# Third attention of an eight-stage kernel: the mask written into PSUM by ScalarE instead of added by 16 identity products a batch

## The reference, cut to what matters

```python
def _L2_xattn_ref(x, cond, mask, wq, bq, wk, bk, wv, bv, wo, bo):
    q = _w8a8_linear(x, wq, bq)            # 8-bit quantised rows times quantised weights
    k = cond @ wk.T + bk ; v = cond @ wv.T + bv      # 16 heads of 16 channels
    scores = jnp.einsum('bhnd,bhld->bhnl', q, k) * inv_sqrt_d + mask[:, None]
    attn = jax.nn.softmax(scores, axis=-1)
    o = jnp.einsum('bhnl,bhld->bhnd', attn, v)
    return _w8a8_linear(o, wo, bo)

x = x + jnp.tanh(g_xattn[2]) * _L2_xattn_ref(_layernorm(x, axis=-1), ctx_2048, mask_BxSxS2_ff0, ...)
```

## Time and profile before

| what | value |
|---|---|
| median of 3 runs | 1387.62 us (1384.13 to 1390.42) |
| profiled execution | 1374.32 us, its span 1372.5 us |
| TensorE, share of the span busy | 83% |
| VectorE | 65% |
| ScalarE | 39% |
| GpSimd | 32% |
| mean granted TensorE clock | 0.939 of 2.4 GHz |
| stage 4, first mask product to last batch's last value work | 742.8 us to about 975 us |

### The profile page before, as it was taken

One profiled execution on the slowest core, in us unless ns is written; L12 is line 12 of the kernel. 1 busy time (PEld: TensorE's weight loads), 2 busy tenths in 40 slices (PEclk: granted clock), 3 DMA queues, 4 the chain that ended last, 5 costly groups with the idle time before them and its releaser, 6 DMA issues.

```text
span 1372.5 us, 34438 instructions
## 1 busy us (share of the span) xinstructions
PE 1144.5 (83%) x12364; PEld 902.6 (66%) x12364; DVE 897.8 (65%) x2468; ACT 534.2 (39%) x1013; POOL 434.1 (32%) x943
## 2 busy tenths in 40 slices
PE   4889898984783888879987999998465799999998
PEld 2667676663771444446665676766354699999998
DVE  3656575665555898856665777777556666666665
ACT  2455554554552676630001333322125333333332
POOL 2444465647858887210011111113222100000000
PEclk8999999996995999989998999999789899999999
DMA  5332332403666454310000000000116100000000
GB/s 186 109 110 79 123 100 92 161 19 115 207 197 152 144 149 131 101 62 1 0 0 24 25 15 23 15 23 0 39 29 191 48 2 17 1 15 0 9 6 16
DMA packets 91469, 93.86 MB, mean 68 GB/s; under 512 B 10276, under 2 KB 83380, under 8 KB 90588
## 3 DMA queue, kind: packets, MB, share of 16 engines
q1 hardware_dynamic: 85500, 78.24, 18.3%
q0 software_dynamic: 4992, 13.66, 3.3%
q10 hardware_dynamic: 864, 0.43, 0.1%
HBM read 56.76 MB, written 35.53 MB: 67 GB/s over the span
## 4 chain that ended last, share of the span: by engine, by line
PE 60%; DVE 16%; issue 9%; ACT 6%; DMA 4%; POOL 3%; SPq 1%; DVEq 1%; ACTq 0%; POOLq 0%
PE psum L2336 5%; PE psum L1387 4%; PE psum L1389 4%; PE psum L1388 4%; PE psum L1012 3%; DMA PT<-xs 2%; DVE mx L782 2%; PE psum L2091 2%; ACT PT L2034 2%; ACT ext L2043 2%; PE psum L1405 2%; PE psum L1407 2%; PE psum L944 2%; PE psum L1406 2%; PE psum L2076 2%
## 5 line engine op out<-in xcount | busy, mean ns | idle before, releaser
L685 POOL TENSOR_SCALAR veps<-mv 128x1 f32<-128x1 f32 x112 | 26.8, 239 | 684.9 <-DVE mv L1255 367.4
L1387 PE MATMUL psum<-xnTh,w7h 128*128 128x256 f32 x512 | 147.1, 287 | 0.0
L1389 PE MATMUL psum<-xnTh,w7l 128*128 128x256 f32 x512 | 145.8, 285 | 0.0
L1388 PE MATMUL psum<-xnTl,w7h 128*128 128x256 f32 x512 | 145.7, 285 | 0.0
L782 DVE TENSOR_REDUCE mx<-psum 128x6 f32<-128x960 f32 (+3 forms) x80 | 80.7, 1008 | 68.8 <-PE psum L980 67.7
L1464 ACT ACTIVATE sil<-psum 128x256 f32<-128x256 f32 x128 | 49.3, 385 | 189.4 <-PE psum L1389 189.4
L1487 DVE TENSOR_TENSOR hTf<-sil,psum 128x256 f32<-128x256 f32 x128 | 53.8, 420 | 97.7 <-ACT sil L1464 97.6
L1389 PEld LDWEIGHTS psum<-xnTh,w7l 128*128 128x128 f32 x512 | 99.1, 193 | 0.0
L1387 PEld LDWEIGHTS psum<-xnTh,w7h 128*128 128x128 f32 x512 | 98.8, 193 | 0.0
L1388 PEld LDWEIGHTS psum<-xnTl,w7h 128*128 128x128 f32 x512 | 98.7, 193 | 0.0
L869 ACT ACTIVATE PT<-psum 128x1024 f32<-128x1024 f32 x64 | 65.5, 1024 | 71.0 <-PE psum L1000 71.0
(11 more groups left out here) (359 smaller groups left out, 3183.3 us busy)
## 6 DMA issues: line engine op xcount, KB each, us to landing
xs<-qpad SPq DMA_DIRECT2D x17, 1024.0 KB, 5.1
ctxT<-in_ctxT SPq DMA_DIRECT2D x48, 128.0 KB, 2.2
ext<-qscr SPq DMA_DIRECT2D x96, 64.0 KB
w_raw<-in_w SPq DMA_DIRECT2D x16, 384.0 KB, 3.3
arena<-in_w SPq DMA_DIRECT2D x4, 1280.0 KB, 9.9
PT<-xs SPq DMA_DIRECT2D x39, 128.0 KB, 2.6
ys<-yt SPq DMA_DIRECT2D x39, 128.0 KB, 2.8
q_parts<-kscr SPq DMA_DIRECT2D x66, 64.0 KB, 2.2
```

The lines of the kernel that those rows point to most:

```text
L1387: MM(o, wh, xnTh[:, s, c], start=(c == 0), stop=False)
L1388: MM(o, wh, xnTl[:, s, c], start=False, stop=False)
L1389: t = MM(o, wl, xnTh[:, s, c], start=False, stop=(c == NC - 1))
```

## The change

TensorE no longer has `add_mask`, GpSimd no longer splits the mask, and the identity in the product's type is gone. ScalarE gets `lay_mask(s, which, k)`, a copy of the mask, spread over 8 heads, from SBUF into two banks at once. It is called four times a batch: twice after the maxima are taken (`which` 1, the transposed mask, for the second scores of the same batch), and twice right after the exp of the same banks (`which` 0, for the first scores of the next batch). So that the score products with `start=False` add to what ScalarE wrote, four products of identities with `start=True` go over banks 4 to 7 once at the start of the stage. The flag `msk` now counts the four copies, and the transfers for batch b+2 wait for the fourth of batch b.

```diff
-        mskp = sb("mskp", [128, 2, 2, 2, T], F32R)
-        ident_r = sb("ident_r", [128, 128], F32R)
-        sb("pad", [128, 896])
+        sb("pad", [128, 2048])
...
-                    sp.wait_ge(F("msk").sem, F("msk").at(b, 2))
+                    sp.wait_ge(F("msk").sem, F("msk").at(b, 4))
...
-            def split(b, s, turn, wait=True):
...
-                P.tensor_copy(mskp[:, s, :, 0], msk[:, s]).then_inc(F("msk").sem, 1)
-                pool.wait_ge(F("msk").sem, F("msk").at(b, 1))
-                P.tensor_tensor(mskp[:, s, :, 1], msk[:, s], mskp[:, s, :, 0].bitcast(F32), ALU.subtract).then_inc(F("msk").sem, 1)
...
+            pool_stage(4, pool)
...
+            def lay_mask(s, which, k):
+                A.copy(bank(4 + 2 * k, 2).rearrange("p (h t) -> p h t", t=T), msk[:, s, which].unsqueeze(1).to_broadcast([128, 8, T])).then_inc(F("msk").sem, 1)
+
             def first():
+                act.wait_ge(wprep_pe, 2)
+                wait("msk_loaded0", 0, 32)
+                for k in range(2):
+                    lay_mask(0, 0, k)
                 copy_x(0)
...
             def body(p, b, n, s, turn, turn_b):
                 if p is not None:
                     copy_values(p)
+                for k in range(2):
+                    wait("mx", b, k + 1)
+                    lay_mask(s, 1, k)
                 wait("st", b, 1)
+                if n is not None:
+                    wait(f"msk_loaded{1 - s}", turn, 32)
                 for k in range(2):
                     A.activation(PT[:, 1024 * k:1024 * (k + 1)], bank(4 + 2 * k, 2), ACT.Exp).then_inc(F("p").sem, 1)
                     if k == 0 and n is not None:
                         copy_x(n)
+                if n is not None:
+                    for k in range(2):
+                        wait("p", b, k + 1)
+                        lay_mask(1 - s, 0, k)
                 if n is not None:
                     copy_k(n, 1 - s)
...
-            def add_mask(s, which, k):
-                for r in (2 * k, 2 * k + 1):
-                    for part in range(2):
-                        MM(bank(4 + r), ident_r[:], mskp[:, s, which, part].unsqueeze(1).to_broadcast([128, 4, T]), start=(part == 0), stop=False, skip_group_check=True)
...
             def first():
+                for r in range(4):
+                    t = MM(bank(4 + r), identb[:], identb[:].unsqueeze(1).to_broadcast([128, 4, 128]), start=True, stop=True)
+                t.then_inc(wprep_pe, 1)
                 transpose_x(0)
...
                 wait("msk", b, 2)
-                for k in range(2):
-                    wait("p", b, k - 1)
-                    add_mask(s, 0, k)
                 wait("k", b, 2)
...
-                for k in range(2):
-                    wait("mx", b, k + 1)
-                    add_mask(s, 1, k)
                 wait("mparts", b, 4)
...
                 wait("mxT", b, 1)
+                wait("msk", b, 4)
...
-                V.tensor_copy(ident_r[:], ident[:]).then_inc(G.sem, 1)
-                dve.wait_ge(G.sem, 2)
```

More of the change, by code:

```diff
@@ L379, in bass_program @@
         ff_flags(3)
-        stage_flags(4, LN + [("ctx_loaded0", 16, 0), ("ctx_loaded1", 16, 0), ("msk_loaded0", 32, 0), ("msk_loaded1", 32, 0), ("msk", 2, 0), ("quant", 6, 0), ("xT_psum", 1, 0), ("xT", 1, 0), ("q_psum", 1, 0), ("k_psum", 1, 0),
+        stage_flags(4, LN + [("ctx_loaded0", 16, 0), ("ctx_loaded1", 16, 0), ("msk_loaded0", 32, 0), ("msk_loaded1", 32, 0), ("msk", 4, 0), ("quant", 6, 0), ("xT_psum", 1, 0), ("xT", 1, 0), ("q_psum", 1, 0), ("k_psum", 1, 0),
                              ("qdve", 3, 0), ("k", 2, 0), ("qT_psum", 1, 0), ("qT", 1, 0), ("sq", 1, 0), ("mx", 2, 0), ("mparts", 4, 0),
-                             ("mxT_psum", 1, 0), ("mxT", 1, 0), ("st", 1, 0), ("p", 2, 2), ("pv", 1, 0), ("pvc", 1, 0), ("pvT", 1, 0), ("rden", 1, 0), ("on", 1, 0),
+                             ("mxT_psum", 1, 0), ("mxT", 1, 0), ("st", 1, 0), ("p", 2, 0), ("pv", 1, 0), ("pvc", 1, 0), ("pvT", 1, 0), ("rden", 1, 0), ("on", 1, 0),
                              ("oquant", 6, 0), ("oT_psum", 1, 0), ("oT", 1, 0), ("y", 1, 0), ("fin", 2, 0)])
@@ L2142, in s4_sp @@
                     sp.wait_ge(F("k_psum").sem, F("k_psum").at(b, 1))
-                    sp.wait_ge(F("msk").sem, F("msk").at(b, 2))
+                    sp.wait_ge(F("msk").sem, F("msk").at(b, 4))
                     load(i * 2 + (u + 2), u)
         def s4_pool(pool):
-            F = lambda n: f[4, n]
-            P = nc.gpsimd
-            rs = rstd_step(4, pool)
-            def split(b, s, turn, wait=True):
[L2153 to L2157, removed]
-                P.tensor_copy(mskp[:, s, :, 0], msk[:, s]).then_inc(F("msk").sem, 1)
-                pool.wait_ge(F("msk").sem, F("msk").at(b, 1))
-                P.tensor_tensor(mskp[:, s, :, 1], msk[:, s], mskp[:, s, :, 0].bitcast(F32), ALU.subtract).then_inc(F("msk").sem, 1)
[L2162 to L2169, removed]
+            pool_stage(4, pool)
         def s4_dve(dve):
@@ L2588, in _ @@
                 A.copy(k_parts[:, s, :, :, 48:64], k_const[:].rearrange("p (c h r) -> p c h r", c=2, h=HK0)).then_inc(gates_ready, 1)
-            give(act, [(4, "p")])
             s0_act(act)
@@ L2646, in _ @@
                 V.tensor_scalar(fb[:], fb[:], gates[:, 6:7], None, ALU.mult).then_inc(G.sem, 1)
-                dve.wait_ge(G.sem, 3)
+                dve.wait_ge(G.sem, 2)
                 s5_dve(dve)
```

## The result

| kernel | median | range | ratio to before (95% interval) |
|---|---|---|---|
| before | 1386.62 us (4 runs) | 1384.13 to 1390.42 | |
| changed | 1414.08 us (4 runs) | 1406.83 to 1414.72 | 1.0193 (1.0150 to 1.0237) |

The change makes the kernel slower by 27 us, 1.9%. A fifth run of the changed kernel, not among the four, took 1419.18 us.

The account below looks back on a forecast made before the run. Stage 4's chain of waits, 13.70 us a batch, was taken as the bound. Constant-clock terms of +1.3 and a falling clock of +21 took the profiled 1374.3 to 1397 us, the median from 1387.6 to 1410; range 1384 to 1431.

Parts of the forecast that it names:

- Price of a copy: Each 128x1024 float32 mask copy by ScalarE from SBUF into PSUM, four a batch: taken as 1.02 us.
- both bounds: Limits for one ScalarE mask copy: 0.59 us from a half-size copy below, 1.2 us from VectorE's pass above.
- the rival that needed a copy of 0.7 or less: Clock holds and ScalarE's copy into PSUM is cheap: total falls by about 8 us, 1377 at 0.6; chance 0.08.
- Leg A: Stage 4, end of second scores to first maxima: 7.8 us in place of 7.34, +0.45 a batch.
- Leg B: Stage 4, first maxima to end of next second scores: 6.1 us at constant clock, -0.25 a batch.
- The sum at constant clock: Both legs over the stage's batches plus the first batch: +6.8, -4.0 and -1.5, making +1.3 us.
- the -1.5: First batch of stage 4: scores stand behind the query's 0.59 us copy, not 2.12 of mask; -1.5 us.
- The clock: Stage 4: granted clock falls in four batches of five, 1.4 us a batch on average, 21 us in all.
- The pause: TensorE idle between the values and the turned maxima: 3.0 us in every batch of stage 4.
- the smaller gap: TensorE idle before the output product, waiting for ScalarE's output copy: 1.2 us a batch, given no cost.
- That the clock holds (1389): Stage 4 keeps full clock through all or nearly all batches: +1.3 us, 1389, between 1384 and 1395; chance 0.19.
- That it stays low throughout (1434): Clock falls and stays low over most of stage 4: 3.0 us a batch, 45 more, 1434; chance 0.1.

Follow-up runs that it names:

- both gaps filled: Changed kernel plus thrown-away TensorE products, eight before the turned maxima and four before the output product: 1375.38 us on another chip, 1.0002 of before.
- the table of two by two: Four kernels against before: ScalarE copies, pause open +27.5 us, filled with eight products +0.5; no copies or mask, open -2.3, filled -17.2.
- the reordered kernel with eight products: Changed kernel with one first-mask copy moved last in ScalarE's row, plus eight thrown-away products before the turned maxima: 1384.64 us, 0.9983 of before.
- the reordered kernel alone: Changed kernel with one first-mask copy kept ahead of the output's copy and the other moved last in ScalarE's row: 1401.74 us, 1.0119 of before.
- the kernel with four products: Changed kernel plus four thrown-away identity products on TensorE between the values and the turned maxima: 1391.34 us, 1.0031 of before.
- that with eight: Changed kernel plus eight thrown-away identity products on TensorE between the values and the turned maxima: 1387.40 us, 0.9994 of before.
- The two kernels in the new order: Changed kernel, one first-mask copy last in ScalarE's row, eight products before the turned maxima: 0.9983 of before; with six more before the first scores: 0.9922.
- the last two experiments: Changed kernel with eight and four added products, 1375.38 us; version with one first-mask copy last and eight and six added, 1363.72 us; both on another chip.

## Why the prediction was right

**The forecast** was 1410 us, and 1414.08 was measured: +27 where +22 was foretold. Between the two profiled executions stage 4 grew by 20.8 us. The prediction put the profile's 13 us below the median aside without a reason; the traces place 12 of them ahead of stage 4, so setting the same +22 on either was right.

**Price of a copy.** 1.02 was taken from the exp; 64 copies took 1.029 each. It lies far from both bounds, and so falls the rival that needed a copy of 0.7 or less.

**Leg A.** Predicted 7.8, with `oT` on ScalarE's queue as the new wait; 7.75 in the batch shown, and 7.70 on average. The steps match too, from the end of the second scores: the query's copy ends at 5.42 (5.40 foretold), the output product starts at 4.99 (4.97), `update` at 5.42 (5.39), the statistics end at 7.82 (7.79). The first scores start at 5.72 and not at 5.45, which costs nothing since VectorE isn't ready.

**Leg B at full clock.** Predicted 6.1, and 6.21 measured with both gaps filled:

```profile
857.33 2.36 DVE L2204 TENSOR_REDUCE mx<-psum 128x8 f32<-128x1024 f32 x2
...
861.38 1.06 PE L2388 MATMUL psum<-mxq,w_attn 96*128 96x128 bf16 x16
862.36 1.17 PE L2391 MATMUL psum<-qT,k_parts 32*128 32x128 f32 x32
```

So 0.15 us a batch were gained there and not 0.25. A whole batch is 13.91, and 13.9 was the sum, since leg A came out 0.1 shorter and leg B 0.1 longer than predicted; that these two cancel is luck. The second pair of copies is hidden, as foretold.

**The sum at constant clock** was +1.3 us. The kernel with both gaps filled shows 1.0002 of before (0.9983 to 1.0021), which is -2 to +3 us. The first batch's second scores end 20.0 us behind the stage ahead in that kernel and 21.5 before, which agrees with the -1.5. The gain of 17 us that the products' removal holds and the 18 us that the copies' place takes are shown by the table of two by two.

**The clock.** The pause was put at 3.0 us and is 2.78 in the batch shown, and 1.7 to 2.8 in the others; the clock of the stage is 0.80. The price was put at 1.4 us a steady batch and is 15.46 - 13.91 = 1.55. Over all fifteen steps from the first second scores to the last, the changed kernel takes 230.1 us and the kernel with both gaps filled 210.4: 19.8 us in the trace, where 21 was foretold. The 5 us by which the timed median lies above the forecast are not in this trace. It is the quickest of the five runs (clock 0.910; the other four, 1413.73 to 1419.18 us, had 0.905 to 0.909), and what the others did in stage 4 isn't recorded. I had let one batch in five escape. In the profiled execution the second scores of the eleven steady batches from 792 us on took 2.02 to 2.07 us in eight, and less in three, one of which ran at full speed. The chain of waits, start and length:

```profile
887.68 1.48 PE psum L2386 x32
...
917.85 1.75 PE psum L2386 x32
...
932.41 1.15 PE psum L2386 x32
```

That the empty pause is the cause, and not what goes with it, is shown by two kernels: filling it brings the time back with the copies in place, and opening it without any copy makes the clock fall. The sentence drawn from the Trainium skill (TensorE: Matmul & The Clock Gate, section HAM oscillation), that the price comes once an iteration, is borne out by the trace after: leg B is longer than 6.21 in eleven of the twelve steady batches.

**What the prediction missed.** It named the smaller gap, 1.2 us before the output product, and gave it no part. In the changed kernel the main pause hides its effect, but the experiments show that once the main one is filled, the clock falls behind the smaller one. It costs little there (14.07 against 13.91 us a batch). In the reordered kernel the smaller gap is another, 1.65 us before the first scores, and filling it is the difference between 0.9983 and 0.9922 of before, 8 us. My expectation of the reordered kernel with eight products failed at this step; that of the reordered kernel alone failed at the price of a fall in leg B, 1.6 us and not 1.1.

**The rivals.** That the clock holds (1389) is refuted by the granted clock. That it stays low throughout (1434) is refuted by the query and key products of the projection, which took 290 and 284 ns each on average, as before (286 and 284); the clock came back before them, though not before the values' projection ahead of them (410 ns each before, 503 after). The argument against it was too strong: dense pieces do not have full clock everywhere, since the `sel4` products and the second scores ran without a gap at 1.2 GHz (and 2.77 of 3.00 us busy went with 0.50 in the earlier trace rows). The range's upper end stood for 2.2 us lost in every batch, by its own terms 1422 us and not 1424. Leg B lost that much in four of the twelve.

**Left open.** Why the kernel with four products is as near to that with eight as it is. Whether what counts is the gap or the work that TensorE has around it: filling a pause changes both, and no kernel leaves the main pause open and has the eight products elsewhere. The two kernels in the new order come nearest: with eight products in the main pause the clock still fell at the first scores, and with six more just ahead of these it didn't. The kernel with the second mask by ScalarE varies from 1388 to 1400 us between runs, and only the mean clock was read with the times, not the batches that fell. Whether a useful piece of work (the turned maxima's neighbours, or part of the next projection) could take the place of the thrown-away products wasn't tried.

## What to carry to other kernels

Work taken off TensorE that stood between two waits leaves a pause, and in a loop that pause may bring the granted clock down for the products behind it, once each time round. So ask of each removed product what it was beside, and price what follows it at both levels. Work given to an engine that runs its list in order is to be placed behind what others wait for: here the same four copies cost 18 us in one place and, with one of them moved and both gaps filled, gave a kernel faster by 0.8%. And a change that ends even may still hold its gain: a kernel with the cost left out, and one with the pause filled, show both parts in four runs.

## What the runs showed of the hardware that was not expected

ScalarE's copy of 128x1024 float32 from SBUF to PSUM, spread from 128 columns by a stride of zero, took 1029 ns, and its exp of the same size from PSUM to SBUF 1032 ns. The Trainium skill, page ScalarE: Activation LUTs, section Step-by-step: what each stage is for, calls the way to PSUM the faster one; at this size no difference is to be seen here. It is no clean comparison, since the two differ in their source and in the function as well.

Eight products a batch whose result nobody reads made a kernel faster, by 27 us with the copies (1414.08 to 1387.40) and by 15 without the mask (1384.63 to 1369.72).

The kernel before took 1387 us on two chips and 1374 on that of the last two experiments, at the same mean clock of its core (0.938), so only ratios within one chip are compared. The traces place most of that difference in the first stage, whose code is the same in all: TensorE starts the second stage at 332 to 333 us in the profiled executions of the kernel before and of the last two kernels, and at 340 to 347 in the other nine. What makes the first stage longer isn't known.
